# Second self attention: where the query projection of the next pair of heads stands in the order of all engines

## The reference, cut to what matters

```python
qkv = einsum('bsh,oh->bso', hidden_states, w_qkv)   # 32 query heads, 4 key heads, 4 value heads of 64
q, k = _rope(q, pos), _rope(k, pos)
k, v = repeat(k, 8), repeat(v, 8)                   # 8 query heads share one key and value head
scores = einsum('bqhd,bkhd->bhqk', q, k) * 64 ** -0.5
attn = softmax(where(causal, scores, min))
out = einsum('bhqk,bkhd->bqhd', attn, v)
return einsum('bso,ho->bsh', out, w_o)              # added to x
```

## Time and profile before

| what | value |
|---|---|
| median of three runs | 2568.33 us |
| the profiled execution | 2568.98 us, span 2567.2 us, granted clock 0.943 |
| from the first mask of pair 0 to that of pair 15 (2197.68 to 2431.19 us) | 233.51 us |
| of that, PE / DVE / ACT / POOL busy | 198.17 / 161.84 / 71.32 / 31.57 us |

### The profile page before, as it was taken

The page is one execution under the profiler, slowest core; times in us unless marked ns, Lnnn a source line. Parts: engine busy times, 40 slices in busy tenths (PEclk is TensorE's granted clock), DMA queues, the critical chain, the costliest instruction groups (busy, mean ns, idle before and its releaser), DMA issues. The chain is left out here.

```text
span 2567.2 us, 45868 instructions
## 1 busy us (share of the span) xinstructions
PE 2280.6 (89%) x16206; PEld 1805.9 (70%) x16212; DVE 1631.9 (64%) x2618; ACT 1206.5 (47%) x2236; POOL 1033.1 (40%) x718
## 2 busy tenths in 40 slices
PE   4589999999997799978988999999999988888766
PEld 2577777777774688866766788888888866666644
DVE  3547877787776333335532688888888874676663
ACT  1346565665652233323203676676667653333242
POOL 3049888988884000000110355455445550110320
PEclk8699999999997899988998999999999998999879
DMA  3000000001000222103312000000000002111200
GB/s 110 1 26 27 27 2 27 27 27 46 4 2 1 80 65 65 53 14 89 77 35 94 26 25 11 20 27 19 18 18 27 1 12 85 46 37 33 79 1 17
DMA packets 104280, 89.92 MB, mean 35 GB/s; under 512 B 32752, under 2 KB 82432, under 8 KB 104080
## 3 DMA queue, kind: packets, MB, share of 16 engines
q1 hardware_dynamic: 103792, 87.28, 11.3%
q0 software_dynamic: 288, 0.00, 0.0%
HBM read 86.22 MB, written 1.05 MB: 34 GB/s over the span
## 5 line engine op out<-in xcount | busy, mean ns | idle before, releaser
L2258 POOL TENSOR_TENSOR xT<-xT,x1b_ring 128x512 f32<-128x512 f32 (+1 forms) x176 | 248.4, 1411 | 213.4 <-ACT x1b_ring L2388 206.5
L923 POOL TENSOR_TENSOR x0b_krstd<-x0b_krstd,minus_half 128x24 f32<-128x24 f32 x64 | 267.0, 4171 | 91.4 <-DVE x0b_krstd L986 85.4
L943 POOL TENSOR_TENSOR xT<-xT,x0b_ring 128x512 f32<-128x512 f32 (+1 forms) x170 | 240.4, 1414 | 38.4 <-ACT x0b_ring L1160 24.3
L111 DVE TENSOR_TENSOR x1b_plo<-x1b_ring,x1b_phi 128x512 fp32r<-128x512 f32 (+1 forms) x208 | 221.8, 1066 | 6.4 <-issue 4.6
L2403 ACT ACTIVATE x1b_ring<-x_ps,x1b_keymask 128x512 f32<-128x512 f32 (+1 forms) x208 | 143.1, 688 | 132.1 <-DVE xT L2330 126.8
L1160 ACT ACTIVATE x0b_ring<-x0b_ring 128x512 f32<-128x512 f32 (+1 forms) x208 | 131.2, 631 | 151.8 <-DVE x0b_ring L1004 143.7
L1036 DVE TENSOR_TENSOR x0b_ring<-x_ps,x0b_krstd 128x512 f32<-128x512 f32 (+1 forms) x208 | 142.8, 686 | 74.1 <-PE x_ps L828 72.0
L116 PE MATMUL x_ps<-x1b_qy,x1b_yT 128*128 128x512 f32 (+1 forms) x416 | 175.7, 422 | 4.3 <-ACT x1b_ring L2403 2.9
L116 PE MATMUL x_ps<-x1b_phi,x1b_yv 128*128 128x512 f32 (+1 forms) x416 | 166.6, 400 | 1.5 <-ACT x1b_out_sb L2370 1.5
L2330 DVE SCALAR_TENSOR_TENSOR xT<-x_ps,x1b_keymask,xT 128x512 f32<-128x512 f32 (+1 forms) x176 | 131.2, 746 | 57.6 <-PE x_ps L118 56.7
L117 PE MATMUL x_ps<-x1b_qy,x1b_yT 128*128 128x512 f32 (+1 forms) x416 | 164.5, 395 | 0.0
(11 more groups left out here) (588 smaller groups left out, 5737.9 us busy)
## 6 DMA issues: line engine op xcount, KB each, us to landing
x_y<-in_ctx_dram SPq DMA_DIRECT2D x8, 1536.0 KB
x_y<-in_ctx_dram SPq DMA_DIRECT2D x24, 512.0 KB, 3.9
a_wn<-in_L_attn_W_Q_dram SPq DMA_DIRECT2D x16, 256.0 KB, 3.0
a_wn<-in_L_attn_W_K_dram SPq DMA_DIRECT2D x16, 256.0 KB, 3.5
a_wn<-in_L_attn_W_V_dram SPq DMA_DIRECT2D x16, 256.0 KB, 4.0
a_won<-in_L_attn_W_O_dram SPq DMA_DIRECT2D x16, 256.0 KB, 2.9
x1a_wq<-in_L_xattn_Wq_dram SPq DMA_DIRECT2D x4, 1024.0 KB, 10.5
x1c_wo<-in_L_xattn_Wo_dram SPq DMA_DIRECT2D x8, 512.0 KB, 7.3
```

Source lines behind the costliest of these rows:

```text
L111: return v.tensor_tensor(lo, exact, hi.bitcast(F32), ALU.subtract)
L923: ins = g_.tensor_tensor(r, r, c.minus_half[:, 0:8].unsqueeze(1).broadcast_to([P, whole, 8]), ALU.pow)
L943: g_.tensor_tensor(total[half][0:m, :], old, src, ALU.add).then_inc(summed, 1)
L2258: g_.tensor_tensor(total[half][0:m, :], old, src, ALU.add).then_inc(summed, 1)
```

## The change

In all texts Q moves from the window's end to the place behind F1, ahead of G, S and V (and C). In the second window B and Q both stand ahead of G, A1 and S, and V now follows S directly. In the prologue it is the same, and G of the second window moves behind Q. The last part's text for the pair 15 is the same as before, without a Q. Because ACT now fills `plain` earlier, two waits on ACT for `rotated` are added ahead of the copy, each asking for a rotation of an earlier window, and one raise of the counter `apart`. The bank of each operation follows from its new place in the list.

```diff
-        HEAD = "N R1 R0 W O F0 F1 G S V C Q"
-        INNER = "N R0 W O F0 F1 G S V Q"
-        TAIL = "N R0 W A0 O F0 F1 G A1 S"
+        HEAD = "N R1 R0 W O F0 F1 Q G S V C"
+        INNER = "N R0 W O F0 F1 Q G S V"
+        TAIL = ("N R0 W A0 O F0 F1", "Q G A1 S V")
...
             if part == "prologue":
-                return (window(1, "A0 A1 W") + window(2, "B") + window(1, "Q") + window(2, "R1 R0 W G S C Q")
-                        + window(3, "N R0 W G F0 F1 S V Q"))
+                return (window(1, "A0 A1 W") + window(2, "B") + window(1, "Q") + window(2, "R1 R0 W Q G S C")
+                        + window(3, "N R0 W F0 F1 Q G S V"))
             if part == "body":
-                return (window(0, INNER) + window(1, TAIL) + window(2, "B") + window(1, "V Q") + window(2, HEAD)
+                return (window(0, INNER) + window(1, TAIL[0]) + window(2, "B") + window(1, TAIL[1]) + window(2, HEAD)
                         + window(3, INNER))
...
                         if op in "BQ":
+
+                            if op == "B" and part != "prologue":
+                                act.wait_ge(rotated, rotation_no(part, i, off, 1) - PAIRSR + 1)
+                            if op == "Q" and not (part == "prologue" and off < 4):
+                                act.wait_ge(rotated, rotation_no(part, i, off - 2, 0) + 2)
+                            act.sem_inc(apart, 1)
                             act.activation(plain[2 if op == "B" else u][:, :], src, ACT.Copy).then_inc(done, 1)
```

## The result

The changed kernel takes 2631.84 us (median of 4 runs, 2631.41 to 2635.12) against 2570.61 us for the kernel before (4 runs, 2560.31 to 2585.69). The ratio is 1.023, with a 95% interval of 1.0194 to 1.0266: slower by 61 us by the medians. The forecast was 2618 us, with a range of 2596 to 2643.

A forecast was written before the change was run, and what follows sets the result against it. DVE's ring was taken to bound the kernel, with Q now waiting for it ahead of S. From the profiled 2568.98 us, +45.2 at full clock and +5 for PE's clock gave 2619, forecast as 2618 us, range 2596 to 2643.

The forecast's parts named there:

- What bounds the kernel: DVE's ring from scores through exponential, zT, N, rotation, W and G to scores closes; PE's wait for plain lies beside it.
- Rival (a): PE sets the pace and its 18.1 us wait for plain was real time: 2550 us, faster; chance 0.04.
- Q waits for `wT lo`, and S for Q: INNER window: Q waits for DVE until 11.60 us after the window's first mark, plus 0.3; the next mark follows 5.18 later.
- The sign foretold for it: In the trace after, PE waits for wT lo ahead of Q, 1 us and more per pair.
- 45.2 at full clock: Added time over the stage: body 39.8, prologue 4.3, pair 1 2.3, last two pairs -1.2 us.
- 5 for the clock: Allowance for PE running slow after idle gaps: 5 us, with bounds 0 to 26 for Q or B, 0 to 20 for O.
- 5.18: Time in us from Q's start to the mark, by ACT's copies of Q and woT hi; by PE it was 4.85.
- 0.49: Time in us by which one ACT copy follows another, used for woT hi queued behind the copy of Q.
- The step that put the mark at the later of two queues: After Q's start, scores end at 4.85 us by PE, the mark comes at 5.18 by ACT; the later counts.
- (b): Only Q's own length counts, as wT lo comes early enough and Q follows F: +28, 2596 us; chance 0.09.
- (c): PE spends gaps at half clock, O and Q run slow in most windows: 35 instead of 5, 2648 us; chance 0.09.
- POOL's term of 0: POOL's straight, now beside woT lo and the mask, slows no DVE work: 0 us, bounds 0 to 5.6.

The follow-up runs named there:

- b_less: Kernel before, with the row maximum taken over every 16th score only: 2555.2 us, ratio 0.9939 to the kernel before.
- a_qs: Changed kernel with Q moved from ahead of G and S to directly behind S, still ahead of V: 2582.2 us, ratio 1.0057 to the kernel before.
- a_fill: Changed kernel plus 16 matmuls of zeros on PE ahead of O in every window: 2638.1 us, ratio 1.0274 to the kernel before.

## Why the prediction was right

**What bounds the kernel.** Right. The shorter maximum speeds up both kernels, and extra PE work in the wait for `plain` is free in the windows where nearly all of that wait lies. Rival (a) fails by both; it holds only for the window behind C, for 2.5 of the 18.1 us. HEAD was named as nearly PE's ring; b_less shows that DVE is on it.

**Q waits for `wT lo`, and S for Q.** The times of the steps came out: `wT lo` T + 11.61, TAIL's B at T + 13.17, HEAD's Q at T + 13.95. That Q stands ahead of S and G is the cause of some 50 us (a_qs). But the forecast's stress on `wT lo` was too heavy: with it out of the way only some 10 us come back, because O at a low clock ends about as late. The sign foretold for it, PE idle ahead of Q in every pair, came in HEAD and in pair 1, in TAIL ahead of B in the first round, and hardly in the INNER windows, where PE came to Q only when F was done.

**Terms that were mis-sized.** To the last mark 62.7 us more were measured, against 45.2 at full clock and 5 for the clock. Pair 0's mark came 5.8 later, of which 1.2 lie ahead of the stage and 4.6 in it (forecast 4.3); pair 1 +4.2 (2.3), body +51.0 (39.8), last two +1.8 (-1.2). Most of the difference is the clock: 12 us by the estimate above, where 5 was taken. It lies in HEAD's Q, in pair 1's Q (7.3 us from Q to mark) and in the last two windows. The total fell inside the range because the range was wide enough for the clock; the single value of 5 for it was too small.

At full clock the sum was short by only 4 us, and three terms in it were off. From Q to the mark it was 5.47 to 5.64 us in place of 5.18. Of that, 0.17 is the added waits and the raise on ACT, which were taken as 0 "as ACT idles before these copies". In the code they stand between ACT's wait for PE and the copy, so the idle time doesn't hide them: the copy starts 3.21 us behind Q's start instead of 3.04, with Q itself as long as before. A run without them was not made. The other 0.3 is that ACT starts `woT hi` 0.71 to 0.78 behind the copy of Q and not 0.49. Against both, the hand-over from `wT lo` to Q was 0.1 to 0.2 us where PE was free, not 0.3.

The 0.49 was read from two `pT` copies, which follow each other directly. Behind each copy to `plain` stands a wait for that copy and a raise, in the kernel before too, and where another copy followed at once there, it also started 0.76 behind:

```profile
2245.14 0.58 ACT L2805 ACTIVATE a_plain<-a_ps 128x512 f32<-128x512 f32 x1
2245.90 0.60 ACT L2816 ACTIVATE a_zT0hi<-a_ps 128x512 fp32r<-128x512 f32 x1 [0.18 <-ACT a_plain L2805]
```

So the row for this term was in the trace before.

**The queue on ACT.** The step that put the mark at the later of two queues was right, but its difference was read as 0.3 us (5.18 against 4.85); it was 1.05. The run with G ahead of Q shows what hung on it: with `woT lo` out of the end of the ring S follows Q directly, and the window is 1.5 us shorter. The path by PE was priced with G inside it, which the other order hides in the wait for `wT lo`.

**Rivals.** (b), Q's own length alone, would have been 2596. In most INNER windows Q did follow F and not `wT lo`, as it says, but only because O was slow; F was done after T + 12, and its price took T + 10.4. (It also calls TAIL shorter and then prices it at 22.3, which is the forecast's.) (c), half clock in most windows, 2648: the clock was below full in every window of the changed kernel's body (0.81 to 0.93), as it says, but the estimate above gives it 8 us in the body and 12 in all, not 35, since much of the slow work lies beside the wait for `wT lo`. POOL's term of 0 stands as a cost: `woT lo` and the mask, its new neighbours, keep 0.69 us in every row above. It was even a small gain: before, three multiplications beside `straight` took 1.06 to 1.26 us in the body, after, none did, which is the 1.5 us between DVE's 132.09 and 130.57.

## What to carry to other kernels

Before moving work ahead of a dependent step, follow it through every engine's queue: what it waits for itself, and whose copies it now stands in front of. A wait that is long in the list of waits is worth nothing if another engine's ring closes around it. Ask it window by window: here the shortest of the waits was the one that counted. Put other work into such a wait (C behind Q, 1.2 us per window) instead of pulling its producer forward past the critical step. And two operations that both precede the critical one are not equal: the one whose result needs two more engines (G) goes first. For the price of a hand-over look for a row of the same pair of instructions, not of a similar one.

## What was unexpected about the hardware

Filling a gap on PE with zeros was no safe remedy here: the zeros ran slow themselves (5.68 us for 16 at a granted clock of 0.73, 4.21 at 1.00) and the slow stretch showed up behind another operation. The clock in the body rose from 0.86 to 0.94 at the same time of 2631 us.

What a low clock costs depends on what stands beside the slow work. In the kernel before, the jump's window took 13.75 and 13.96 us at a clock of 1.00 and 15.16 at 0.89. In the changed kernel it took 17.8 to 18.5 us at 0.81 to 0.90, and with zeros 17.8 at 1.00 (a_fill, two rounds): O's slow matmuls are mostly covered by the wait for `wT lo`. The mean of the granted clock over a stage doesn't tell these two cases apart; the windows do.
